# Six dt projections made a chunk ahead in pairs of row groups, with 12 scan buffers in place of 16

## The reference, cut to what matters

```python
D_MODEL, D_STATE, EXPAND = 384, 16, 2          # D_INNER = 768, DT_RANK = 24
xin, z = split(xseq @ in_proj_w.T)             # 768 columns each
u   = silu(causal_conv3(xin) + conv_b)
dbc = u @ x_proj_w.T                           # 24 columns for dt, 16 B, 16 C
dt  = softplus(dbc[:, :24] @ dt_proj_w.T + dt_proj_b)
h_t = exp(dt_t * A) * h_{t-1} + (dt_t * u_t) * B_t      # 768 x 16 states, 1024 steps
y_t = sum_n h_t[:, n] * C_t[n]
out = ((y + u * D) * silu(z)) @ out_proj_w.T
```

## Time and profile before

| | |
|---|---|
| median of 3 runs (lowest, highest) | 3620.64 us (3618.16, 3621.16) |
| profiled execution: time, span | 3612.3 us, 3610.5 us |
| mean granted TensorE clock | 0.973 |
| busy, share of the span: PE, DVE, ACT, POOL | 92%, 88%, 74%, 71% |
| the 16 chunks, 960 drives of POOL | first scan at 69.9 us, last scan ends at 2623.4 us |
| a scan on DVE, without and with a carry in | 1204 to 1216 ns, 1264 to 1271 ns |
| a drive or a multiply on POOL | 1280, 1278 ns |
| a decay on ACT; an exp of 128x512 to `slot` | 689, 711 ns |

### The profile page before, as it was taken

The page is one execution under the profiler, slowest core; times in us unless marked ns, Lnnn a source line. Parts: engine busy times, 40 slices in busy tenths (PEclk is TensorE's granted clock), DMA queues, the critical chain, the costliest instruction groups (busy, mean ns, idle before and its releaser), DMA issues. The chain is left out here.

```text
span 3610.5 us, 49832 instructions
## 1 busy us (share of the span) xinstructions
PE 3324.0 (92%) x16962; PEld 2349.5 (65%) x16962; DVE 3191.6 (88%) x3280; ACT 2663.0 (74%) x5126; POOL 2573.6 (71%) x2045
## 2 busy tenths in 40 slices
PE   6999989999999999999999999998879998889997
PEld 3666666666666666666666666666657786567776
DVE  3999999999999999999999999999967887876886
ACT  4877887787878778877877887787655555875653
POOL 3899999989998998999999899999901101551100
PEclk7999999999999999999999999999999999999998
DMA  4020211202020220202021120202210123650212
GB/s 145 2 94 21 93 54 50 86 18 86 19 103 28 77 86 19 86 19 102 22 83 69 35 86 19 94 10 94 70 45 35 54 84 119 252 193 18 71 37 88
DMA packets 83585, 249.88 MB, mean 69 GB/s; under 512 B 15213, under 2 KB 24045, under 8 KB 73093
## 3 DMA queue, kind: packets, MB, share of 16 engines
q1 hardware_dynamic: 82564, 245.65, 18.8%
q10 hardware_dynamic: 768, 1.05, 0.1%
HBM read 204.73 MB, written 41.95 MB: 68 GB/s over the span
## 5 line engine op out<-in xcount | busy, mean ns | idle before, releaser
L957 POOL TENSOR_TENSOR slot<-dtu,b_rep 128x512 f32<-128x512 f32 x960 | 1214.7, 1280 | 106.6 <-PE ysum L457 106.5
L967 POOL TENSOR_TENSOR slot<-slot,c_rep 128x512 f32<-128x512 f32 x864 | 1099.5, 1278 | 65.4 <-ACT carry L763 57.5
L754 ACT ACTIVATE state<-dt,aneg 128x512 f32<-128x512 f32 x960 | 656.9, 689 | 248.4 <-DVE slot L1061 177.0
L457 PE MATMUL ysum<-ident,slot 128*128 128x128 f32 x6144 | 808.7, 277 | 17.1 <-POOL slot L967 16.9
L457 PEld LDWEIGHTS ysum<-ident,slot 128*128 128x128 f32 x6144 | 713.5, 144 | 156.8 <-issue 134.0
L1053 DVE TENSOR_TENSOR_SCAN slot<-state,slot 128x512 f32<-128x512 f32 x384 | 456.1, 1204 | 57.7 <-ACT state L754 57.7
L1053 DVE TENSOR_TENSOR_SCAN slot<-state,carry,slot 128x512 f32<-128x512 f32 x384 | 478.2, 1264 | 0.0
L575 PE MATMUL state<-diag_b,dtu_t 128*128 128x128 f32 x3072 | 420.6, 281 | 54.5 <-ACT carry L763 41.3
L575 PEld LDWEIGHTS state<-diag_b,dtu_t 128*128 128x128 f32 x3072 | 383.3, 194 | 129.4 <-issue 128.7
L1061 DVE TENSOR_TENSOR slot<-state,c_rep 128x512 f32<-128x512 f32 x672 | 447.2, 667 | 0.0
L745 ACT ACTIVATE slot<-dt,aneg 128x512 f32<-128x512 f32 x576 | 404.6, 711 | 2.8 <-PE ysum L457 2.7
(11 more groups left out here) (268 smaller groups left out, 5925.8 us busy)
## 6 DMA issues: line engine op xcount, KB each, us to landing
c_rep<-rows_of_b_and_c SPq DMA_DIRECT2D x64, 1024.0 KB, 4.7
xres_l<-between_layers SPq DMA_DIRECT2D x18, 1536.0 KB, 10.0
xn_l<-between_layers SPq DMA_DIRECT2D x13, 1536.0 KB, 6.4
...
```

The costliest lines, as they stand in the source:

```text
L457: last = mm(ysum[:, cols], slot[:, (NS * k + n) % SLOTS, cols], ident[:], start=first and j == 0, stop=final, is_transpose=True, skip_grou ...
L754: af(state[:, (NS * k + n) % BANKS], dt[:, k], ACT.Exp, scale=aneg[:, k, n:n + 1]).then_inc(exp_done, 1)
L957: tt(slot[:, q % SLOTS], dtu[:, k % 2], b_rep[:, b_row(n)], ALU.mult).then_inc(dbu_done, 1)
L967: tt(slot[:, q % SLOTS], slot[:, q % SLOTS], c_rep[:, n], ALU.mult).then_inc(pool_mult_done, 1)
```

## The change

All six dt products of a chunk are made in the chunk before it. `x_proj` now has 88 weight columns: the 24 dt columns stand twice, at 0 and at 64, so that `xp` holds the dt part in rows 0 to 23 and again in rows 64 to 87, and `w_dt` is loaded twice in the same way. The products go in three pairs, the first of a pair on rows 0 to 23 into px, the second on rows 64 to 87 into py. Tiles 4 and 5 have two places in `dt` each, used in turn. One softplus block (two activations) stands at ACT's step 80. `SLOTS` goes from 16 to 12 and `POOL_LAG` from 9 to 5, and most tables of places have new numbers. `b_runs` gives the same four transfers of B as before, since `PE_N` is the same.

```diff
-SLOTS = 16
+SLOTS = 12
-POOL_N, POOL_LAG = (0, 1, 2, 4, 5, 8, 9, 10, 12), 9
-PE_N, TURN_N, SCALE_AHEAD, SCALED = (5, 7, 11, 13, 14, 15), (11, 13), 5, 2
-SUM_AT = (3, 4, 8, 6, 11, 11, 8, 12, 13, 14, 13, 14, 15, 16, 14, 16)
+POOL_N, POOL_LAG = (0, 1, 3, 4, 5, 7, 9, 10, 11), 5
+PE_N, TURN_N, SCALE_AHEAD, SCALED = (5, 7, 11, 13, 14, 15), (11, 13), 6, 2
+SUM_AT = (5, 3, 8, 4, 11, 11, 8, 12, 13, 14, 15, 14, 16, 16, 14, 16)
-OUT_AT, OUT_PER = (0, 4, 12), (3, 3, 1)
+OUT_AT, OUT_PER = (0, 6, 12), (3, 3, 1)
-MEAN_AT, CENTER_AT, SQUARE_AT, VAR_AT, RSTD_AT, SCALE_AT = 75, 87, 91, 88, 94, 95
+MEAN_AT, CENTER_AT, SQUARE_AT, VAR_AT, RSTD_AT, SCALE_AT = 76, 79, 90, 90, 95, 95
...
-SILU_AT = (31, 45, 57, 80)
-SOFT = ((4, 6), (), (), (0, 4))
-XP_AT, XP_COPY_AT = 54, 60
-DT_AT, DT_IN = (57, 60, 64, 69, 1, 19), (BX, BY, BZ, BX, BZ, BZ)
-DT_READ_AT = (62, 65, 75, 76, 8, 26)
-EARLY = 4
-DT_U_AT = 13
-TURN_U_AT, COPY_U_AT = (91, 8, 28, 45, 61, 78), (95, 20, 33, 50, 67, 83)
+SILU_AT = (31, 43, 57, 80)
+SOFT_AT = 3
+XP_AT, XP_COPY_AT = 53, 62
+DT_AT, DT_IN = (59, 61, 67), (BX, BY, BX, BY, BX, BY)
+DT_READ_AT = (64, 65, 66, 71, 74, 75)
+DT_U_AT = 1
+TURN_U_AT, COPY_U_AT = (87, 14, 31, 45, 60, 75), (95, 17, 36, 49, 69, 84)
...
+def dt_tile(c, k):
+    return k if k < GROUP else k + 2 * (c % 2)
...
+            for row in DT_ROWS:
+                sp.dma_start(w_x[:, :, row:row + DTR], xw[:, :, 0:DTR]).then_inc(x_w_in, 16)
+                sp.dma_start(w_dt[row:row + DTR], dt_wT).then_inc(dt_w_in, 16)
...
+            def dt_proj(d, pair):
+                if pair == 0:
                     pe.wait_ge(xp_read, d + 1)
                     if later(d):
                         pe.wait_ge(z_read, KT * (d - 1) + 4)
+                        pe.wait_ge(gated, KT * (d - 1) + 3)
+                else:
+                    pe.wait_ge(dt_read, KT * d + 2 * pair)
+                for m in (2 * pair, 2 * pair + 1):
+                    rows = slice(DT_ROWS[m % 2], DT_ROWS[m % 2] + DTR)
+                    mm(pg[DT_IN[m]][:], w_dt[rows, m * P:(m + 1) * P], xp[rows, :], start=True, stop=True).then_inc(dt_full, 1)
...
+            def softplus(d):
+                act.wait_ge(dt_read, KT * (d + 1))
+                for tiles in (slice(0, GROUP), slice(dt_tile(d, GROUP), dt_tile(d, KT - 1) + 1)):
+                    af(dt[:, tiles], dt[:, tiles], ACT.Softplus).then_inc(dt_done, tiles.stop - tiles.start)
```

More of the change, by code:

```diff
@@ L108, in b_rows, with b_runs @@
     return [n for n in range(GROUP * j, GROUP * (j + 1)) if n not in PE_N]
+def b_runs(j):
+    rows, runs = b_rows(j), []
+    while rows:
+        by = rows[1] - rows[0] if len(rows) > 1 else 1
+        n = 1
+        while n < len(rows) and rows[n] - rows[n - 1] == by:
+            n += 1
+        runs.append((rows[0], by, n))
+        rows = rows[n:]
+    return runs
 class Lead:
@@ L417, in gate_proj @@
                 if k == 5:
[L418 to L421 removed]
+                    pe.wait_ge(u_copied, KT * c + 5)
                 for t in range(CT):
@@ L524, in turn_u @@
                 if k == 1:
-                    pe.wait_ge(dt_read, KT * c + 5)
+                    if later(c):
+                        pe.wait_ge(gated, KT * c)
+                    else:
+                        pe.wait_ge(u_copied, 1)
                 if k == 2:
@@ L608, in scan @@
                     for k in range(KT):
-                        if q == DT_AT[k] and (after or k >= EARLY):
-                            dt_proj(d if k < EARLY else c, k)
                         if q == GATE_AT[k]:
@@ L614, in scan @@
                             in_proj(d, 1 - h, k)
+                    for pair in range(KT // 2):
+                        if after and q == DT_AT[pair]:
+                            dt_proj(d, pair)
                     if c == 0 and q == FIRST_NORM_AT[0]:
@@ L639, in _ @@
                 in_proj(0, 0, m)
-            pe.wait_ge(x_w_in, 32)
+            pe.wait_ge(x_w_in, 48)
             pe.wait_ge(gap_set, 1)
             x_proj(0, 0)
-            pe.wait_ge(dt_w_in, 16)
-            for m in range(EARLY):
-                dt_proj(0, m)
+            pe.wait_ge(dt_w_in, 32)
+            for pair in range(KT // 2):
+                dt_proj(0, pair)
             turn_b(0)
@@ L870, in scan @@
                     for k in range(KT):
-                        if q == DT_READ_AT[k] and (after or k >= EARLY):
-                            dt_read_tile(d if k < EARLY else c, k)
+                        if after and q == DT_READ_AT[k]:
+                            dt_read_tile(d, k)
                     for k in range(KT):
@@ L882, in scan @@
                                 gate_silu(c, k)
-                            if SOFT[g] and (after or SOFT[g][0] >= EARLY):
-                                softplus(d if SOFT[g][0] < EARLY else c, *SOFT[g])
+                            if after and g == SOFT_AT:
+                                softplus(d)
                             nc.scalar.preload_act_table_set("natural_log_exp_and_others")
@@ L903, in _ @@
             store_bc(0, 0)
-            for m in range(EARLY):
+            for m in range(KT):
                 dt_read_tile(0, m)
-            softplus(0, 0, EARLY)
+            softplus(0)
             nc.scalar.preload_act_table_set("natural_log_exp_and_others")
```

83 lines of the change are left out of this document (30 added, 53 removed).

## The result

The changed kernel takes 3676.48 us (median of 4 runs, 3671.93 to 3680.5), the kernel before in the same session 3620.11 us: a ratio of 1.0159 [1.0147, 1.0172], 56 us slower. Forecast was 3589 us. The profiled execution has a span of 3670.1 us (3610.5 before) at a mean granted clock of 0.965 (0.973).

The account below looks back on a forecast made before the run. A chunk takes DVE's work plus its waits. Even chunks 4.7 us off, odd 0.1 on, eight times each, 4.4 once later: 32 us off, profiled execution 3580, median 8.3 above it: 3589 us; range 3552 to 3640.

Parts of the forecast that it names:

- I judge the change by what it does to these places: Prices the change at DVE's existing waits in an even chunk: q = 7, 11, 32, 76 and 81.
- the sum: All terms together: even chunks 4.7 us off, odd 0.1 on, eight times each, 4.4 once later; 32 us off.
- part 1: One softplus group, ACT's steps 31 and 80: even chunk gains 2.3 and about 0.5 us, odd loses 1.3.
- part 3: Two more convolution places, ACT's block from 45 to 43: waits of 1.3 and 0.3 us gone, nearly all even chunks.
- part 2: dt products off PE's chunk start: 1.6 us less at q = 7 to 11, even keeps 1.0, odd 1.5; pairs count 0.
- part 4: 12 buffers and lag 5 on POOL: small shortages cost 0.7 us an even and 0.3 an odd chunk; bounds 0 and 4.5.
- rival (c): Block at ACT's step 80 costs 4 us, not 2, as centering waits for a late mean; 3620 us; chance 0.13.
- The sum would stay as it is, because nothing there ends last: Even if whole products of a dt pair overlapped on PE (1.2 us a pair), the forecast time would not change.
- rival (a): POOL becomes the bound: DVE waits 3.5 us a chunk for its drives, 14 us slower, 3635 us; chance 0.22.

Follow-up runs that it names:

- e17: e10 with the squares moved from step 90 to 91; ratio 1.0009 [1.0, 1.0019] to the kernel before, 3621.37 us.
- e5: Changed kernel with normalisation near its old places, first turn of u at 91, last two gate products two steps earlier, third dt pair at 64; 1.0081.
- e10: e5 with the centering at step 79 and the squares at 90; ratio 1.0043 to the kernel before.
- e13: Changed kernel with the centering alone put back from step 79 to 87; ratio 1.0177 to the kernel before.
- e6: Changed kernel with both products of a dt pair on rows 0 to 23, so that nothing can overlap; ratio 1.0223 to the kernel before.
- e12: Kernel before with lag 5 and 12 buffers, nothing else changed; ratio 1.0055 to the kernel before.
- e2: Kernel before with the changed kernel's lag, sums and POOL states, but 16 buffers; ratio 1.0288 to the kernel before.
- e8: Changed kernel with normalisation near its old places, first turn of u at 91, softplus of tiles 4 and 5 back at ACT's step 31; 1.0163.

## Why the prediction was wrong

**The step that failed** is "I judge the change by what it does to these places", the places where DVE waited before. At those places (q = 0 to 16, 30 to 56, 76 to 78, 80 to 83) the table has 5.2 us less in an even chunk and 0.2 less in an odd one; the sum had 5.4 (2.3 + 0.5 + 1.0 + 1.6) and 0.2 (1.5 - 1.3). In total they came out as forecast, but by luck in part: 0.6 us too much in part 1 and 0.8 in part 3 against 1.2 too little in part 2 of an even chunk. At all the others, where DVE had hardly waited and for which the sum held 0.7 and 0.3 us (part 4), it has 6.4 us more in even and 5.1 more in odd chunks. The changed tables move the last two gate products from steps 68 and 72 to 72 and 74, the squares and the variance from 91 and 88 to 90, the turn of u from 91 to 87 and the copy of B from 87 to 91, and none of these moves had a price; the late mean was weighed only in rival (c). They were in the change. The sum also took PE's clock as it was: a chunk has 8.0 us at 1.2 GHz in place of 4.0, an estimated 1.8 us of the 3.62.

**The shares.** New places for the work at the end of the chunk win nearly all of it back: from the changed kernel to e17, which differs in them alone (the normalisation, the last two gate products, the third pair with its reads, the first turn and a copy of u), it is 1.0159 to 1.0009, 54 us. Some of these places are the old ones, others are new, so 54 us is what the places can give, and not what each move had cost. It is not a sum of parts: the centering alone gains nothing and the variance alone loses 27 us. The move of the gates and the pair gains nothing by itself (e5), with the centering at 79 another 14 us go (e10), with the squares at 91 another 12 (e17).

**Part 1** was nearly right. The wait at q = 32 is gone. Its reckoning of the block, decay 81 ready 9.4 us after the multiply, with 7.4 us of DVE's work in between, gives 2.0 us with the centering and 3.7 without: e10 has 1.9 and 1.8, e5 3.68 and 3.40. In the changed kernel it is 2.8 and 2.5 on average, which hides two cases. In the seven chunks of chunks 2 to 13 where the mean's products run at the full clock it is 1.8 to 2.1 us, the 2.0 of the forecast; in the other five it is 3.4 to 3.7, since they run at the lower clock (4.36 us in place of 2.84). What DVE waits for is the mean and not the decay, as rival (c) had it, but (c) had no word on the clock. The mean's load is issued no earlier than before, while DVE gets there 3.5 us sooner. e13, which takes the late mean off the path, gained nothing, and the time of (c), 3620, was 56 us short.

**Part 2.** The waits at q = 0 to 16 fell by 2.2 us in both kinds of chunk (1.6 forecast, of which 1.0 and 1.5 kept), and 1.7 and 0.6 us came back at q = 17 to 29, half of it in even chunks and all of it in odd ones at q = 23 for a drive of L585. The pair was put at 1.6 us and takes 1.05: whole products run side by side. By the rule of "TensorEngine Tiling (Array Packing)" (Key Properties) in the Trainium skill they would, and the trace agrees. "The sum would stay as it is, because nothing there ends last" is wrong by e6: 0.83 us less per pair, 2.5 per chunk, are worth 23 us. PE stood 0.67 us at the second pair in even chunks and 0.47 in odd ones, less than the 1.5 to 2 forecast.

**Part 3.** The waits for the convolution input are gone (1.4 us of an even chunk; 0.55 for a decay at q = 44 is in their place), but the small one at q = 58 grew from 0.4 to 1.3.

**Part 4 and rival (a).** DVE waits 1.9 us in 2000 for POOL, so (a) did not come. Yet lag and buffers are not free: 20 us in e12, in the old order, where part 4 had 0.7 and 0.3 us a chunk, about 8 us. They reach DVE as later drives of PE (L572 and L575 together 64.2 us in place of 47.1) and later decays (34.7 in place of 29.6), and not as a wait for POOL. What they cost in the changed kernel no run shows.

**Open.** How much of the loss is PE's lower clock and how much the waits ahead of it: no run holds one of them fixed. The 0.58 us a chunk in the distances of scans: e2, with the new states and nothing else new on DVE, has 1134.3 and 1188.5 ns, 0.35 us of it; the rest wasn't tried. How much 16 buffers would give in the changed kernel: no run has them. Why e8 waits at q = 84 to 95. e17 equals the kernel before per chunk (159.68 and 159.85 us), and its 7 us more of span are 4.5 of a later first scan, 2 in the 16 chunks together and 1 behind them. No version is faster than the kernel before.
